# Opening of a two-layer graph kernel: Wh copied by two engines in turn, two of eight products on ScalarE, denominator columns on GpSimd, x transposes first

## The reference, cut to what matters

```python
# N = 8192 nodes, 128 features, adj: 8192 x 8192 int32 of 0 and 1
Wh = x @ W
e = (Wh @ a1)[:, None] + (Wh @ a2)[None, :]
e = where(e > 0, e, 0.2 * e)
e = where(adj > 0, e, -9e15)
x1 = layernorm(x + elu(softmax(e, axis=1) @ Wh))
out = layernorm(x1 + concat([adj @ x1 / deg, x1]) @ weight + bias)
```

## Time and profile before

| what | us |
|---|---|
| three runs | 1485.79, 1486.53, 1487.88; median 1486.53 |
| span of the profiled execution | 1484.3 |
| median less that span, what lies around it | 2.2 |
| PE busy | 1449.9 (98%) |
| DVE busy | 994.9 (67%) |
| ACT busy | 936.4 (63%) |
| POOL busy | 118.3 (8%) |

### The profile page before, as it was taken

The page is one execution under the profiler, slowest core; times in us unless marked ns, Lnnn a source line. Parts: engine busy times, 40 slices in busy tenths (PEclk is TensorE's granted clock), DMA queues, the critical chain, the costliest instruction groups (busy, mean ns, idle before and its releaser), DMA issues.

```text
span 1484.3 us, 33988 instructions
## 1 busy us (share of the span) xinstructions
PE 1449.9 (98%) x12110; PEld 1107.8 (75%) x12110; DVE 994.9 (67%) x2833; ACT 936.4 (63%) x2289; POOL 118.3 (8%) x199
## 2 busy tenths in 40 slices
PE   7599999999999999999999999999999999999998
PEld 7578888888888888888888888884454545454557
DVE  4998888888788888878887887773433343334332
ACT  6989999999999999999999999940000000000000
POOL 1001000100010010001000100000000000000000
PEclk9799999999999999999999999999999999999999
DMA  9969997788788868877886882041000000000000
GB/s 174 111 71 101 120 108 90 83 94 95 84 86 96 93 78 95 94 90 82 95 94 83 87 96 37 19 119 49 22 15 21 14 21 14 21 14 21 14 15 15
DMA packets 99201, 101.47 MB, mean 68 GB/s; under 512 B 4432, under 2 KB 66384, under 8 KB 99152
## 3 DMA queue, kind: packets, MB, share of 16 engines
q0 software_dynamic: 33792, 67.11, 45.5%
q1 hardware_dynamic: 64800, 33.57, 8.7%
q10 hardware_dynamic: 560, 0.14, 0.1%
HBM read 289.48 MB, written 12.65 MB: 204 GB/s over the span
## 4 chain that ended last, share of the span: by engine, by line
PE 90%; DMA 2%; DVE 1%; issue 0%; POOL 0%; ACT 0%; SPq 0%; DVEq 0%; POOLq 0%
PE acc L679 58%; PE pack_ps L758 27%; PE pack_ps L819 2%; DMA adj_space<-in_adj 2%; PE acc L793 1%; PE pack_ps L628 1%; PE turn_ps L780 1%; PE turn_ps L769 0%; DMA level_ring<-x_rows 0%; DMA x_parts<-parts 0%; POOL one L378 0%; DVE adj_space L945 0%; DVE stats L1118 0%; DVE part_sums L1051 0%; DVE edge_ring L1020 0%
## 5 line engine op out<-in xcount | busy, mean ns | idle before, releaser
L466 ACT ACTIVATE level_ring<-s_row,cols 128x256 fp8e4<-128x256 f32 x1984 | 803.7, 495 | 0.0
L679 PE MATMUL acc<-factors,edge_ring 128*128 128x259 f16 x4096 | 548.8, 274 | 14.5 <-DVE edge_ring L1020 13.0
L679 PE MATMUL acc<-factors,level_ring 128*128 128x259 f16 x4096 | 548.3, 274 | 0.0
L758 PE MATMUL pack_ps<-adj_space,factors 128*128 128x512 fp8e4 x1920 | 421.7, 379 | 0.9 <-issue 0.9
L679 PEld LDWEIGHTS acc<-factors,edge_ring 128*128 128x128 fp8e4 x4096 | 365.9, 98 | 64.8 <-issue 15.8
L679 PEld LDWEIGHTS acc<-factors,level_ring 128*128 128x128 fp8e4 x4096 | 366.5, 98 | 48.9
L758 PEld LDWEIGHTS pack_ps<-adj_space,factors 128*128 128x128 f16 x1920 | 187.9, 98 | 217.6 <-issue 1.1
L1013 DVE TENSOR_TENSOR level_ring<-level_ring,edge_ring 128x1024 uint16<-128x1024 uint16 x256 | 171.2, 689 | 103.7 <-ACT level_ring L466 93.3
L1190 DVE TENSOR_SCALAR adj_space<-words 128x512 uint16 (+1 forms) x448 | 96.3, 288 | 146.7 <-PE pack_ps L758 146.6
L628 PE MATMUL pack_ps<-pack_w,adj_space 128*128 128x32 bf16 x960 | 170.7, 178 | 0.0
L1020 DVE TENSOR_TENSOR edge_ring<-edge_ring,level_ring 128x1024 uint16<-128x1024 uint16 x256 | 166.7, 683 | 0.1
(11 more groups left out here) (104 smaller groups left out, 726.8 us busy)
## 6 DMA issues: line engine op xcount, KB each, us to landing
adj_space<-in_adj POOLq DMA_DIRECT2D x64, 1024.0 KB, 14.5
rows_x<-in_x SPq DMA_DIRECT2D x32, 128.0 KB, 2.1
x_rows<-rows_y SPq DMA_DIRECT2D x32, 128.0 KB, 9.7
x_parts<-parts SPq DMA_DIRECT2D x32, 128.0 KB, 4.4
factors<-x_parts SPq DMA_DIRECT2D x8, 512.0 KB, 4.8
level_ring<-x_rows SPq DMA_DIRECT2D x16, 256.0 KB, 2.8
out<-level_ring SPq DMA_DIRECT2D x32, 128.0 KB, 1.8
s_row<-s_and_t SPq DMA_DIRECT2D x30, 128.0 KB, 3.0
```

The source lines that it names most:

```text
L466: a = act.activation(level_bytes[:, h % MASK_SLOTS, j, :], s_row[:, slot, :], ACT.Relu, bias=t_big[:, h * HALF + j:h * HALF + j + 1], scal ...
L679: m = pe.matmul(acc[a][:, 0:WIDE_ROW], mask, factors[:, neg, jj, 0:WIDE_ROW], start=(jj == 0), stop=(jj == NJ - 1))
L758: m = pe.matmul(pack_ps[slot][:, :], factors[:, 0, jj, part * F:(part + 1) * F], ring_1_bytes[:, c, j, :], start=(jj == 0 and part == 0), ...
```

## The change

The edits all lie in the opening and in group 0.

- PE transposes x blocks 0 and 1 before the small product of W and a (which goes to another PSUM tile). `pack_bits(0)` stands ahead of the last block of Wh.
- ACT copies only the even blocks of Wh, DVE the odd ones (`keep_wh`). DVE takes the largest value from PSUM, and the copies of ACT wait for that (`top_ok`).
- ACT makes products 4 and 5 (`make_late_product`), in 16 instructions of 128x128 each, into the part of `factors` that unit 3 takes later; DVE makes the six others. The order of products, masks and low parts on DVE is new, and so is the order on ACT.
- The denominator columns, y and its two multiples go to POOL, in two parts: units 0 to 2 at once, unit 3 when `low_of(4)` and `low_of(5)` are done, because products 4 and 5 lie there until then. All this stands in the queue of POOL ahead of the loads of row block 1.

```diff
+        late_product = [factors[:, k, (UPG - 1) * UNIT:NJ, :].rearrange("p j r -> p (j r)").bitcast(F32)[:, 0:UNIT * F]
+                        .rearrange("p (j f) -> p j f", f=F) for k in range(2)]
+        product_of = [product[:, 0], product[:, 1], product[:, 2], product[:, 0], late_product[0], late_product[1],
+                      product[:, 1], product[:, 2]]
...
+            def denominators(js, n):
+                for k, den in enumerate((e_den, f_den)):
+                    pool.tensor_copy(factors[:, k, js, F], den[:, js]).then_inc(den_hi_ok, 1)
+                    pool.memset(factors[:, k, js, ROW:WIDE_ROW], 1.0).then_inc(edge_col_ok, 1)
+                pool.wait_ge(den_hi_ok, 4 * n + 2)
+                for k, den in enumerate((e_den, f_den)):
+                    pool.tensor_tensor(factors[:, k, js, ROW - 1], den[:, js], factors[:, k, js, F], ALU.subtract)\
+                        .then_inc(den_hi_ok, 1)
+            pool.wait_ge(t_max_ok, 1)
+            pool.tensor_tensor(y_col, s_col, t_max.to_broadcast([P, NJ]), ALU.add).then_inc(y_ok_col, 1)
+            pool.wait_ge(exp_cols_ok, 2)
+            for col, den in ((e_col, e_den), (f_col, f_den)):
+                pool.tensor_scalar(den, col, E_SCALE, None, ALU.mult).then_inc(den_ok, 1)
...
+            denominators(slice(0, (UPG - 1) * UNIT), 0)
...
+            pool.wait_ge(e_low_ok, 3)
+            pool.wait_ge(f_low_ok, 3)
+            denominators(slice((UPG - 1) * UNIT, NJ), 1)
...
             def copy_wh(k):
-                act.wait_ge(wh_ok, k + 1)
+                act.wait_ge(top_ok, k + 1)
...
-                if k:
+                if k % 2:
                     copy_wh(k - 1)
-            copy_wh(NX - 1)
-            act.wait_ge(s_row_ok, 1)
+                    if k > 4:
+                        first_scores((k - 5) // 2, (k - 3) // 2)
+            first_scores(6, 12)
+            copy_words(0, 0)
             act.wait_ge(s_turned, 1)
             act.activation(s_turn, turn_ps[0][:, 0:P], ACT.Copy).then_inc(s_turn_ok, 1)
-            first_scores(0, 2)
+            first_scores(12, 16)
...
+            def make_late_product(k):
+                for j in range(UNIT):
+                    jj = 2 * UNIT + j
+                    a = act.activation(late_product[k][:, j, :], wh[:, jj, :], ACT.Copy, scale=(e_col, f_col)[k][:, jj:jj + 1])
+                a.then_inc(act_product_ok, 1)
...
                 pe.wait_ge(x_t_ok, k + 1)
                 if k >= 2:
-                    pe.wait_ge(wh_copied, k - 1)
+                    pe.wait_ge(wh_ok, k - 1)
+                    pe.wait_ge(top_ok, k - 1)
+                    pe.wait_ge(wh_kept if k % 2 else wh_copied, k // 2)
...
             for k in range(NX):
-                if k + 1 < NX:
+                if 0 < k < NX - 1:
                     turn_x(k + 1)
                 make_wh(k)
...
+                if k == NX - 2:
+                    pe.wait_ge(pack_w_ok, 2 * TILES - 1)
+                    pack_bits(0)
...
             def largest_wh(k):
-                dve.wait_ge(wh_copied, k + 1)
-                dve.tensor_reduce(wh_top[:, k:k + 1], wh[:, XB * k:XB * (k + 1), :], AX.XY,
-                                  ALU.max, apply_absolute_value=True).then_inc(top_ok, 1)
+                dve.tensor_reduce(wh_top[:, k:k + 1], wh_banks(k)[:, :, :, 0:F], AX.XYZ, ALU.max,
+                                  apply_absolute_value=True).then_inc(top_ok, 1)
+            def keep_wh(k):
+                dve.tensor_copy(wh[:, XB * k:XB * (k + 1), :].rearrange("p (h j) f -> p h j f", h=2),
+                                wh_banks(k)[:, :, :, 0:F]).then_inc(wh_kept, 1)
...
+                if k < NX - 1:
+                    if k % 2:
+                        keep_wh(k)
+                    largest_wh(k)
...
+            make_product(0)
+            scale_of_wh()
+            make_product(1)
+            first_masks(0)
+            low_of(0, e_low_ok)
+            make_product(2)
+            low_of(1, f_low_ok)
+            make_product(3)
+            first_masks(1)
+            low_of(2, e_low_ok)
+            low_of(3, f_low_ok)
+            make_product(6)
+            first_masks(2)
+            low_of(4, e_low_ok)
+            low_of(5, f_low_ok)
+            make_product(7)
+            sum_of_x()
```

More of the change, by code:

```diff
@@ L173, in adj_resnorm_kernel @@
         w0_turned, w_turn_ok, wa_made, wa_ok = (sem(n) for n in "w0_turned w_turn_ok wa_made wa_ok".split())
[L174 removed]
+        x_turned, x_t_ok, wh_made, wh_ok, top_ok, wh_kept = (sem(n) for n in "x_turned x_t_ok wh_made wh_ok top_ok wh_kept".split())
         s_turned, s_turn_ok, sum_x_ok, sum_xb_ok = (sem(n) for n in "s_turned s_turn_ok sum_x_ok sum_xb_ok".split())
@@ L593, in _ @@
             pe.wait_ge(w0_in, 16)
[L594 to L598, removed]
-            pe.wait_ge(ones_ok, 1)
+            pe.transpose(pack_ps[0][:, 0:P], wq[:, 0:F], ident).then_inc(w0_turned, 1)
             def turn_x(k):
@@ L652, in _ @@
             turn_x(0)
+            turn_x(1)
+            pe.wait_ge(w_turn_ok, 1)
+            pe.wait_ge(a0_in, 16)
+            pe.matmul(pack_ps[0][:, P:P + 2], w_turn, a_sb, start=True, stop=True).then_inc(wa_made, 1)
+            pe.wait_ge(wa_ok, 1)
             for k in range(NX):
-                if k + 1 < NX:
+                if 0 < k < NX - 1:
                     turn_x(k + 1)
@@ L709, in _ @@
                     pack_bits(c + 2)
+                if c == 2:
+                    pe.wait_ge(sum_xb_ok, 1)
+                    pe.matmul(turn_ps[1][:, 0:F], sum_xb, wq[:, 0:F], start=True, stop=True).then_inc(mean_made, 1)
             group(1, {1: (1, 0), 2: (1, 1), 3: (1, 2)})
@@ L1027, in low_of @@
                 dve.wait_ge(high_ok, n + 1)
-                dve.scalar_tensor_tensor(out=factors[:, k, js, FD:FD + F], in0=product[:, n % 3, :, :], scalar=scale_e,
+                dve.scalar_tensor_tensor(out=factors[:, k, js, FD:FD + F], in0=product_of[n], scalar=scale_e,
                                          in1=factors[:, k, js, 0:F], op0=ALU.mult, op1=ALU.subtract)\
@@ L1154, in group, with first_masks, sum_of_x @@
                 elu_and_residual(g - 1, second)
-            for c in range(UPG - 1):
-                low_of(2 * c, e_low_ok)
-                low_of(2 * c + 1, f_low_ok)
-                masks(0, 0, c)
-                make_product(2 * c + 2)
-                make_product(2 * c + 3)
-            last_masks_of_first()
+            def first_masks(c):
+                dve.wait_ge(mask_used, 2 * c + 2)
+                dve.wait_ge(words_ok, c + 1)
+                unpack(0, 0, c, edge_ring, c).then_inc(unpacked, 1)
+                for k in range(2):
+                    negative(0, c, k)
+                    positive(0, c, k)
+            def sum_of_x():
+                dve.wait_ge(x_t_ok, NX)
+                dve.tensor_reduce(sum_x, x_sums[:, :], AX.X, ALU.add).then_inc(sum_x_ok, 1)
+                dve.wait_ge(sum_x_ok, 1)
+                dve.tensor_scalar(sum_xb, ident, 0.0, sum_x, ALU.mult, ALU.add).then_inc(sum_xb_ok, 1)
+            make_product(0)
[15 more added lines that the diff above has]
+            sum_of_x()
+            dve.wait_ge(mask_used, 2 * UPG)
+            dve.wait_ge(words_ok, UPG)
+            for k in range(2):
+                low_half(2 * UPG - 2, k, e_low_ok)
+                if k == 0:
+                    unpack(0, 0, UPG - 1, edge_ring, UPG - 1).then_inc(unpacked, 1)
+                low_half(2 * UPG - 1, k, f_low_ok)
+                negative(0, UPG - 1, k)
+                positive(0, UPG - 1, k)
             dve.wait_ge(mean_made, 1)
```

114 lines of the change are left out of this document (50 added, 64 removed).

## The result

| | us |
|---|---|
| before, same session | 1487.2 median of 4 runs (1485.79 to 1488.1) |
| after | 1509.34 median of 4 runs (1508.29 to 1510.53) |
| ratio after / before | 1.0147, 95% interval 1.0133 to 1.016 |
| span of the profiled execution after | 1506.6 (before 1484.3) |

Slower by 22.1, where 12.0 was forecast, and 1509.34 lies above the range, which ended at 1505.5. Three windows of after, with the columns of the earlier trace rows, and behind them the last of the three in the kernel before show where to look.

What follows compares the result with a forecast made beforehand. It took group 1's start, set by full ACT and DVE lists, then adjacency loads as the bound. +4.0 blocks, +3.0 queue, +2.2 list made +9.2; loads brought it to +12.0: 1498.5 us, range 1491.0 to 1505.5.

Steps and rivals of the forecast that it cites:

- Step 1: Opening, Wh blocks: pairs slow from 2.66 to 3.54 us through DVE's reduction and ACT's copy; block 14 ends 4.0 later.
- Step 2: ACT's queue after Wh block 14: e_col at 42.2 against 35.19, +7.0 in all, +3.0 beyond the blocks.
- Step 3: ACT's list from exponentials to last high part: grows from 47.0 to 49.2, +2.2; last high part at 91.4.
- the term for the third pack: Group 0: ACT's third word copy waits for PE's pack, 65 to 67.8; less 0.9 earlier idle, +2.
- the +9.2 of steps 1 to 3: Start of group 1: later by +4.0 for blocks, +3.0 for the queue and +2.2 for ACT's list.
- Step 4: Row block 1 loads behind `low_of(5)` on POOL: first leaves at 86.0, row block 2 loads 12 later; total reaches +12.
- POOL is held up: Rival, POOL's denominators: product 7 and slow instructions send loads 4 to 8 later; 1501.5 to 1506 us, chance 0.17.
- DVE's shorter list counts: Rival, exponentials to last mask: DVE saves 5.8, e_col only 1.6 later; -4.2, 1482.3 us, chance 0.05.
- The small prices are low: Rival, reduction, late products and POOL cheap: group 1 at +5.5, loads +7.5; 1491 to 1494.5 us, chance 0.14.

Runs made afterwards that it cites:

- loads_first: The changed kernel, with the four loads of row block 1 ahead of the second denominators on POOL; 1501.4 us.
- pool_copies_only: loads_first, but POOL keeps only the casts and memsets of the denominators and the arithmetic goes to DVE; 1498.0 us.
- den_on_dve: The changed kernel, with the denominators and the four columns of y back on DVE; 1497.9 us.
- den_wh_before: den_on_dve, with the whole Wh stage as before and its 22 scores behind the exponentials again; 1492.5 us.
- den_wh_before_late: den_wh_before, with products 4 and 5 made by DVE; 1488.5 us.
- late_only: The kernel before, and of the change only that ACT makes products 4 and 5; 1494.7 us.
- best: Kernel before; DVE copies Wh blocks 5, 7, 9, 11 and sums x earlier, ACT makes 8 pieces of product 6, group 1's first scores come later; 1485.3 us.
- before_pool_tensor: The kernel before, with an unused memset and six unused 128x64 TENSOR_SCALAR on POOL between its reductions and row block 1's loads; 1485.4 us in one run.
- tops_from_sbuf: The changed kernel, but ACT copies even Wh blocks first and DVE takes the largest of both blocks from SBUF; 1506.8 us.
- before_pool_quiet: before_pool_tensor, with the second to fourth load of adjacency moved behind the six POOL instructions; 1507.5 us.
- before_pool_copies: The kernel before, with an unused memset and six unused 128x64 copies on POOL between its reductions and row block 1's loads; 1487.2 us.

## Why the prediction was right and wrong

The sign was right, the size was not. One chain of kernels, each undoing one thing more, divides the 22.1 (the parts add to 21.8): loads behind the second denominators 8.0 (`loads_first`), the change of configuration and POOL's held-up instructions 3.4 (`pool_copies_only`, in time the same as `den_on_dve`), the Wh stage with its queue 5.4 (`den_wh_before`), the late products 4.0 (`den_wh_before_late`), the order 1.0, which is within its interval. Another sequence would divide it a little otherwise: the late products cost 3.1 where they were undone first. Of the 10.1 that the forecast lacked, POOL's part is 3.4, the loads are 5.2 (8.0 for 2.8), and the rest of the change is 1.4 (10.6 for 9.2).

**Step 1, blocks of Wh**: right. Pairs 3.62 apart for 3.54, PE's wait 0.69 for some 0.8, DVE's reduction and copy from PSUM 0.68 each. (The lower bound for the five pairs should read 4.05, not 3.9.)

**Step 2, queue up to the exponentials**: right. e_col at 43.01 for 42.2, ACT busy up to it. That ACT's queue decides held as far as it went: with the scores behind the exponentials the chain over the last block takes over at once.

**Step 3, ACT's list**: the price of a late product was right (4.77 / 16 = 0.30), and so was its effect, shown by `late_only`. What failed is the term for the third pack, "+2". It took group 0 to wait for `low_of(1)` at 57.7, and gave POOL's first denominators, which group 0 waits for as well, no time at all. They came at 63, the copy waited 8.23, and the last high part ended at 97.7 for 91.4. In `den_on_dve`, where POOL is out of it, that wait is 3.04 (forecast 2.8, from 65 to 67.8) and the kernel 10.6 slower: the +9.2 of steps 1 to 3 hold there within 1.4.

**Step 4, loads**: the mechanism was right, the size not. The six instructions of the second part took 2.9 (89.67 to 92.58), forecast 2.7, but that is luck: product 7 held the first for 2.18, and the other five took 0.9 in all, where the sum had no hold and 0.45 for each. They began 6.4 later than forecast (89.67 for 83.3), because high parts 4 and 5 were late by step 3. That alone does not make the price, since group 1 was late by nearly as much (108.49 for 102.3). The sum let the first load land after 13.0, as one from an idle queue; with four issued at once it took 15.6, and the row with four at once in the earlier trace rows has 14.3. So two joins waited, 2.79 and 2.70, where the sum had one wait of 3.3. The layer norm of group 0 moved with them, and the loads of row block 2 left 20.5 later than before (136.26 for 115.73), forecast 12. Piece (2, 2) followed, as forecast, and PE's stop there brought the lower clock, 1.6, which the sum had nowhere. The forecast gave the loads 2.8 beyond group 1's start; the spans show 7.0, and `loads_first` 8.0.

**The failed steps in two sentences**: in step 3 the first denominators on POOL were costed at nothing, with 0.22 to 0.74 for one instruction and no cost to start; they took 10.76 to start, then some 2.2 for each of four, held group 0 until 63.13 (the sum had it ready at 57.7) and cost 3.4 with the loads out of the way. In step 4 the loads were sized at 2.8 beyond group 1's start and cost 8.0, through two waits for one and a stop of PE at the lower clock.

**Rivals**: "POOL is held up" named one of the two causes on POOL and the direction, but its 1506 did not hold the change of configuration. Its evidence was weaker than it looked: of the long instructions of the earlier trace rows, one at 203.14 (0.54) ran beside DVE's unpacks, which have one SBUF input, and not beside an instruction with two. The hold of the first instruction by product 7 came as the prediction priced it (2.18 for 2.29). "DVE's shorter list counts" fell in `late_only` by waits of 3.71 and 8.96, and "The small prices are low" by 0.30 for a late product.

## What to carry to other kernels

Before work goes to an engine that is idle, look at what that engine ran last, and at what it will have to run next: POOL's change of configuration took 6.7 to 11.4 here, and in the kernel before no row showed its price, since it lay inside a longer wait. Follow each small result to the first instruction that waits for it, also when it is off every list that was summed. When a set of loads moves, take each landing from a row with as many loads at once, and look for a wait at every piece. Of two full engines, taking work from one paid here only where the other, which got it, had been relieved first (`late_only`, `best`).

## What the runs showed of the hardware

- Behind a partition reduction POOL does a memset (0.22) and copies at once, but its first arithmetic instruction waits 10.5 to 11.4 with adjacency loads under way (10.52 in `before_pool_tensor`, 10.76 in after, 11.18 in `loads_first`, 11.41 in `tops_from_sbuf`) and 6.72 without (`before_pool_quiet`).
- A 128x64 copy on POOL took 0.24 at its shortest and 2.29 at its longest, the latter beside a DVE instruction with two SBUF inputs (`before_pool_copies`).
- DVE is slowed as well: four unpacks, with one SBUF input each, took 2.13 in after beside POOL's casts and memsets and 1.79 in `pool_copies_only` beside a cast, a memset and two issues of loads, 0.90 otherwise.
- Behind 3.40 without work PE's first two runs of 8 matmuls took 1.89 and 1.86, behind 0.78 or 0.88 they took 1.05 (after; `loads_first` and before).
